# VectorE's reads of the column jobs' banks move ahead of its sums of states

## The reference, cut to what matters

```python
def step(state, xs):
    d_t, B_t, C_t, u_t = xs
    dA = jnp.exp(d_t[..., None] * A)
    state = dA * state + (d_t * u_t)[..., None] * B_t[:, None, :]
    y_t = jnp.einsum('bdn,bn->bd', state, C_t)
    return (state, y_t)
...
y = jnp.swapaxes(ys, 0, 1) + u * D_param
y = y * jax.nn.silu(gate)
return y @ W_out.T
```

## Time and profile before

| what | value |
|---|---|
| median of 3 runs | 1119.11 us (1116.91 to 1120.78) |
| the profiled execution | 1115.61 us, its span 1113.8 us, 1.8 us around it |
| TensorE busy | 1020.4 us, 92% of the span |
| VectorE busy | 1036.3 us, 93% |
| GpSimd busy | 968.3 us, 87% |
| ScalarE busy | 720.9 us, 65% |
| granted TensorE clock, mean | 0.977 of full speed |
| chain that ended last, by engine | TensorE 31%, GpSimd 27%, VectorE 22%, issue 15%, ScalarE 3% |

### The profile page before, as it was taken

How to read it: one execution, slowest core, us unless ns; L and a number is a source line. 1 busy time by engine, 2 the same in 40 slices (tenths; PEclk the granted TensorE clock), 3 DMA queues, 4 the chain that set the end, 5 groups by cost and what they waited for, 6 DMA issues and landing times.

```text
span 1113.8 us, 14875 instructions
## 1 busy us (share of the span) xinstructions
PE 1020.4 (92%) x5040; PEld 749.4 (67%) x5040; DVE 1036.3 (93%) x1237; ACT 720.9 (65%) x1177; POOL 968.3 (87%) x531
## 2 busy tenths in 40 slices
PE   6979987989989999989989999999999999999767
PEld 4757665667668885666768886675858886555444
DVE  5699999898999999899999999999999999888895
ACT  5767667875666976577576877477676766455440
POOL 3668998999989999699979999779979999879871
PEclk9999998899999999999999999999999999999988
DMA  4647663633334654343334644243333452434410
GB/s 156 216 153 245 227 215 106 215 115 116 100 106 155 219 182 149 114 161 104 104 95 150 222 180 165 100 161 124 113 107 120 174 185 72 135 121 171 136 53 38
DMA packets 46619, 160.93 MB, mean 144 GB/s; under 512 B 5358, under 2 KB 5614, under 8 KB 37072
## 3 DMA queue, kind: packets, MB, share of 16 engines
q1 hardware_dynamic: 46400, 159.93, 41.9%
q10 hardware_dynamic: 144, 0.07, 0.0%
HBM read 135.59 MB, written 24.38 MB: 144 GB/s over the span
## 4 chain that ended last, share of the span: by engine, by line
PE 31%; POOL 27%; DVE 22%; issue 15%; ACT 3%; DMA 0%; SPq 0%; DVEq 0%; POOLq 0%
POOL sb_dBu L912 16%; DVE sb_h L1190 11%; PE pj L1251 8%; PE pj L1463 7%; PE hT L1554 6%; POOL sb_yT L865 5%; DVE sb_yT L1106 5%; PE pj L1528 3%; POOL sb_v L847 2%; DVE sb_un L988 2%; PE pj L1572 2%; POOL sb_u L851 1%; PE pj L1497 1%; PE pj L1256 1%; POOL sb_delta L842 1%
## 5 line engine op out<-in xcount | busy, mean ns | idle before, releaser
L912 POOL TENSOR_TENSOR sb_dBu<-sb_v,sb_bb 128x1024 f32<-128x1024 f32 x254 | 602.7, 2386 | 38.7 <-DVE sb_h L1190 28.7
L1190 DVE TENSOR_TENSOR_SCAN sb_h<-dA,sb_dBu 128x512 f32<-128x512 f32 x512 | 597.9, 1212 | 18.5 <-POOL sb_dBu L912 15.8
L672 ACT ACTIVATE dA<-sb_delta,sb_apar 128x512 f32<-128x512 f32 x510 | 346.0, 691 | 216.9 <-DVE sb_h L1190 215.1
L1251 PE MATMUL pj<-sb_x_hi,sb_w_sp 128*128 128x512 f32 x1208 | 340.0, 405 | 20.6 <-DVE sb_un L988 11.9
L1554 PE MATMUL hT<-sb_ident,sb_h 128*128 128x128 f32 x2048 | 286.4, 282 | 52.5 <-DVE sb_yT L1106 42.1
L1554 PEld LDWEIGHTS hT<-sb_ident,sb_h 128*128 128x128 f32 x2048 | 242.1, 144 | 136.3 <-issue 46.4
L1251 PEld LDWEIGHTS pj<-sb_x_hi,sb_w_sp 128*128 128x128 f32 x1208 | 220.1, 191 | 68.0 <-issue 9.0
L1106 DVE SCALAR_TENSOR_TENSOR sb_yT<-hT,sb_cs,sb_yT 128x512 f32<-128x512 f32 x336 | 239.5, 739 | 18.5 <-PE hT L1554 18.1
L865 POOL TENSOR_TENSOR sb_yT<-sb_yT,sb_part 128x512 f32<-128x512 f32 x140 | 180.2, 1287 | 34.9 <-ACT sb_part L778 34.7
L778 ACT ACTIVATE sb_part<-hT,sb_cs_act 128x512 f32<-128x512 f32 x140 | 96.0, 686 | 107.6 <-PE hT L1554 97.6
L1251 PE MATMUL pj<-sb_x_lo,sb_w_sp 128*128 128x512 f32 x604 | 165.1, 396 | 0.0
(11 more groups left out here) (148 smaller groups left out, 773.2 us busy)
## 6 DMA issues: line engine op xcount, KB each, us to landing
sb_w_sp<-w_cache SPq DMA_DIRECT2D x55, 1024.0 KB, 4.8
sb_ring<-w_ring SPq DMA_DIRECT2D x67, 512.0 KB, 3.8
sb_bb<-b_rows SPq DMA_DIRECT2D x128, 256.0 KB, 3.5
w_cache<-sb_w_sp SPq DMA_DIRECT2D x19, 1024.0 KB, 4.9
sb_xio<-x SPq DMA_DIRECT2D x7, 1024.0 KB, 6.9
out<-sb_xio SPq DMA_DIRECT2D x3, 1024.0 KB, 6.1
sb_xio<-x SPq DMA_DIRECT2D x4, 256.0 KB, 3.4
out<-sb_xio SPq DMA_DIRECT2D x4, 256.0 KB, 2.0
```

The lines of the kernel that those rows point to most:

```text
L672: nc.scalar.activation(dA[g % 2][:, :], delta[:, j, :], ACT.Exp, scale=apar[:, j, n:n + 1]).then_inc(dA_done, 1)
L912: nc.gpsimd.tensor_tensor(dBu[:, dbu_buffer(s), :, :], v[:, j:j + 2, :], bb[:, i % B_RING, :].unsqueeze(1).to_broadcast([P, 2, T]), ALU.mu ...
L1190: nc.vector.tensor_tensor_scan(h[:, i % 2, 2 * part + e, :], dA[g % 2][:, :], dBu[:, dbu_buffer(s), e, :], 0.0, ALU.mult, ALU.add).then_in ...
L1251: done = nc.tensor.matmul(bank[:, :], w[:, kk * P:(kk + 1) * P], xs[:, kk, :], start=(p == 0), stop=(p == len(products) - 1))
```

## The change

In every unit but the first, VectorE calls `side(s)` right after the two scans of the slot and before the sums of states. In unit 0 (slots 0 and 1 of each sequence) the order stays. No instruction is added or removed, no semaphore and no buffer changes, and the programs of the other engines are the same.

```diff
                         nc.vector.tensor_tensor_scan(h[:, i % 2, 2 * part + e, :], dA[g % 2][:, :], dBu[:, dbu_buffer(s), e, :],
                                                      0.0, ALU.mult, ALU.add).then_inc(scan_done, 1)
+
+
+                    if i > 0:
+                        side(s)
                     for c in (2 * part, 2 * part + 1):
                         if i > 0 and c not in handed_over(i - 1, first):
                             add_state(i - 1, c, False)
                         elif i == 0 and not first and c not in handed_over(UNITS - 1, False):
                             add_state(UNITS - 1, c, True)
-                    side(s)
+                    if i == 0:
+                        side(s)
```

## The result

| | before | changed |
|---|---|---|
| median of 20 runs | 1120.44 us (1116.69 to 1125.19) | 1124.13 us (1118.62 to 1130.27) |
| the profiled execution | 1115.61 us, span 1113.8 | 1126.6 us, span 1124.8 |
| granted clock, mean of that execution | 0.977 | 0.970 |

The ratio is 1.0038, 95% interval 1.0021 to 1.0056: some 4.3 us slower where +2.0 us was forecast (the medians lie 3.7 us apart). The sign and the range held; the size was too small, by about half in this comparison. By the prediction's own line of 0.3% the result is "slower", to which it gave 0.32, and not "same", to which it gave 0.55; 1124.13 us lies at the upper edge of the 1118 to 1124 of its case (d).

A forecast was written before the change was run, and what follows sets the result against it. The bound changes hands: GpSimd at seams, VectorE with TensorE close behind, TensorE alone in the output projection, VectorE through the taps. -1.0 + 1.2 + 0 + 1.8 = +2.0 us: 1117.6 profiled, median 1121.1; range 1115.5 to 1126.

The forecast's parts named there:

- the prediction's own line of 0.3%: Whole kernel: 0.3% (3.4 us) is what a measurement can tell from no change.
- slower: Whole kernel: a measured time more than 0.3% above before; chance 0.32.
- same: Whole kernel: a measured time within 0.3% of before; chance 0.55.
- case (d): Whole kernel: the forecast itself, small terms that nearly cancel, 1118 to 1124 us; chance 0.55.
- The seams: Between sequences: GpSimd's step done 0.64 us sooner, net gain 0.34 each; three seams -1.0 us, bounds -4.0 and 0.
- The give-back: Slot 4 behind a seam: VectorE waits for transposes and gives back 0.3 us of the 0.64 gained.
- The entry of the output projection: Slot 24, sequences 1 and 2: sum behind a 0.60 us gate, +1.2 us; slot 25's casts only in upper bound 3.6.
- The taps: Tap stretches: sums 2.24 us later but covered by TensorE's slack; 0, bounds 0 and +1.0 us per sequence.
- Rival (a): Slots 46 to 58 and 7 to 22: delayed sums become a bound, slower, about +5 to +8.0 us; chance 0.22.
- The last sequence: TensorE the bound: entry +0.15, slots 36 to 42 +1.0, slots 50 and 51 +0.6; +1.8 us, bounds 0.6 and 3.0.
- Rival (b): Tap stretches and the wait at 1045: TensorE's clock falls more often, three more falls +5, 1126 us; chance 0.10.
- case (c): Seams: both GpSimd waits go and slot 24's delay finds slack, -4.0 us, 1115.1 us; chance 0.13.

The follow-up runs named there:

- experiment 6: New order in sequences 0 to 2 except slot 24, old order in the last sequence; 1119.92 us against 1120.8 for the kernel of before, ratio 0.9990.
- experiment 11: New order only in slots 40 to 42 of the last sequence; 1124.24 us against 1121.07 for the kernel of before, ratio 1.0023.
- Experiment 10: New order only in slots 50 and 51 of the last sequence; 1122.89 us against 1120.8 for the kernel of before, ratio 1.0018.
- experiment 1: New order in the last sequence alone; 1125.58 us against 1121.4 for the kernel of before, ratio 1.0037.
- experiment 8: New order in sequences 0 to 2 except slots 24 and 25, old in the last; 1119.92 us against 1121.07 for the kernel of before, ratio 0.9980.
- experiment 9: New order in the last sequence except slots 50 and 51; 1124.21 us against 1120.8 for the kernel of before, ratio 1.0028.
- experiment 5: New order only in slots 59 to 62 of the first three sequences; 1121.89 us, ratio 1.0005 to the kernel of before.
- experiment 2: The changed kernel run again, same instructions; 1124.47 us against 1121.4 for the kernel of before, ratio 1.0021.

## Why the forecast had the sign and not the size

**The seams: right, sized a little low.** Forecast -0.34 us each, measured -0.65. The give-back that I took off is there, +0.2 us at slot 5 of sequence 1 (6.44 to 6.65 us against before), but it is gone again by slot 24 (6.44). -1.95 instead of -1.0.

**The entry of the output projection: nearly the right size, for the wrong reason.** I charged the sum of slot 24 behind a gate with 0.6 us and set the casts of slot 25 aside as an upper bound to be added. The experiments turn that round: slot 25 alone costs 0.82, and with both the step is the same 0.82. What slot 24 delays is seen ahead of the first column only (0.94 us of wait for 0.35), and slot 25's delay covers it: two delays of one chain don't add, the later decides. In the changed kernel the two waits grow by 0.59 and 0.22 us, 0.81 in all; with slot 24 left out the second alone is 0.60 (experiment 6), and the step is still 0.82. No run has the new order in slot 24 and not in slot 25, so what slot 24 costs alone is not measured. +1.65 instead of +1.2.

**The taps: right.** Between slots 36 and 60 of sequences 1 and 2 the difference to before moves by less than 0.1 us in every kernel, and the stretch of the earlier trace rows kept its clock. Rival (a) is dead, though the sums were delayed by up to 2.24 us: its other place, slots 7 to 22, shows no loss in the changed kernel either. The Trainium skill ("TensorE: Matmul & The Clock Gate", section on psum-queue depth-cycling) tells of another kernel in which frequent short idle gaps between groups of matmuls make the clock swing. This trace does not show it: TensorE's seven waits for sums in the taps, at most 1.4 us, left it at 1.00, as did before's (five waits, at most 1.5 us).

**The last sequence: the order right, the price of the clock left out.** By the order: -0.07 + 0.45 up to slot 42, 0.59 behind the sum of slot 42 (-1.11 against -1.70, where no half clock falls in either), 0.6 at slots 50 and 51. That is +1.6, forecast +1.8. But +4.1 us was measured for this sequence alone (2.8 to 5.5). The term that I had set to nothing is the clock of the first column behind a wait. In the tail the eight matmuls take 5.3 to 5.8 us in all four traces with the new order in slots 50 and 51, and 4.1 to 4.4 in nine of the ten with the old one (5.61 in experiment 11). Behind slot 42 they take 5.3 to 5.55 in three of five traces with the new order in slots 40 to 42, and in two of nine with the old. Experiment 10 shows 0.6 us of delay and 1.3 of clock behind one edit, in one trace.

**Sum.** Seams -1.95, entries +1.65, last sequence +1.6: +1.3 us by the order, forecast +2.0. The clock adds 1.25 + 1.70 - 0.59 = 2.4 and 2.08 - 0.6 = 1.5 us in both traces of the changed kernel, relative to a trace that has no half clock at slot 43, and the 0.3 us behind slot 63 come on top. That is two executions; on average it must be less. The 32 executions of the changed kernel average 1124.4 us and the 115 of the kernel before in the experiments 1121.1, +3.3 us (standard error 0.6), which leaves about 2.0 for the clock. That is a remainder and no measurement. Nor do the executions show clearly more time at half clock: the mean granted clock of the 32 is 0.9699 and that of 103 of before 0.9706, by 2 x (1 - clock) x time 68 and 66 us at half clock, each with a standard error above 1. The traces show a difference in where the half clock falls. Rival (b) thus named the right mechanism in the wrong form: not more falls in the taps or elsewhere, but falls, longer in these traces, that lie over two columns where nothing covers them. In absolute time the forecast lay 3.0 us low, of which 1.3 are the median of before (1119.11 us of three runs, 1120.44 of twenty). The range was said to reach to case (c), 1115.1, and began at 1115.5; nothing hangs on it.

**What stays open.** Whether half clock falls on slot 43 is not settled by the order alone: three of five against two of nine could be chance. The same holds for the +1.6 to +1.7 us between 3:24 and 3:36 in experiments 1, 8 and 11, where the first column of the output projection takes 5.37 us for 3.67 (experiments 8 and 11), with no wait ahead of it that differs from the other traces with the old order there. No experiment held the clock fixed.

## What to carry to other kernels

An instruction moved ahead of another on an engine that is never late is still not free: look for who waits for the one that was put back. The longest delay need not be the one that costs (2.24 us in the taps cost nothing), nor the nearest (slot 24): here it was slot 25, where 1.78 us of `side` cost 0.82. Count a chain of delays by the last and not by their sum. Where TensorE is the bound, price a delay of its wait by the clock of what follows too: in experiment 10's trace 0.6 us of order became 1.9 us. And before two profiles are subtracted, take off what differs ahead of the first place that the change touches, and run the old kernel again to see which steps are its own.

## What the runs showed of the hardware that was not expected

- The half clock behind a wait is not a fixed price. Behind the same wait of 2.92 us, the next eight matmuls took between 4.08 and 5.76 us in twelve traces. In the other two, experiments 8 and 9, the clock had fallen earlier, the wait was 2.51 and 2.57 us, and they took 4.40 and 4.43. In the two kernels that were traced twice it repeats (5.76 and 5.74 us; 4.27 and 4.20), but the column of slot 42 took 5.29 us in one trace of the kernel before and 3.60 in the other.
- The mean granted clock of the executions of a kernel (eleven or twelve each) differs with the order of a few instructions on another engine: 0.9739 in experiment 8, 0.9706 in 103 executions of before, 0.9666 in experiment 1 and 0.9665 in experiment 5. As time at half clock, 2 x (1 - clock) x time, that is 58, 66, 75 and 75 us (standard errors 1 to 3.5; the two ends of what twelve kernels show). Experiments 1 and 5, with some 9 us more of it than before, both come out some 2.5 us above what the order alone gives: +4.1 for +1.6, and +0.6 for -1.95. The changed kernel has hardly more of it than before and still lies 2 us above its +1.3, so the amount alone does not give the cost.
- Start-up up to slot 4 differed by up to 8.5 us between executions (0 in the profile of before, 8.49 in experiment 2).
